# Perceiver block: expert rows scaled two tiles ahead, gathers issued one per transposed tile, fewer warming products

## The reference, cut to what matters

```python
x = x + _L0_ffn_ref(_layernorm(x, axis=-1), routers, W1, W2)
# _L0_ffn_ref: four times, xt of shape (2048, 128):
logits = xt @ router                      # (2048, 16)
probs = jax.nn.softmax(logits, axis=-1)
w, idx = jnp.max(probs, axis=-1), jnp.argmax(probs, axis=-1)
# over the experts i:
h = jax.nn.silu(xt @ w1) @ w2             # 128 -> 512 -> 128
sel = jnp.where(idx == i, w, 0.0)
acc = acc + sel[:, None] * h
```

## Time and profile before

| | us |
|---|---|
| median of three runs | 706.57 |
| lowest, highest | 699.62, 711.03 |
| profiled execution | 701.39 |
| its span, first to last instruction | 699.6 |

### The profile page before, as it was taken

The page is one execution under the profiler, slowest core; times in us unless marked ns, Lnnn a source line. Parts: engine busy times, 40 slices in busy tenths (PEclk is TensorE's granted clock), DMA queues, the critical chain, the costliest instruction groups (busy, mean ns, idle before and its releaser), DMA issues.

```text
span 699.6 us, 16660 instructions
## 1 busy us (share of the span) xinstructions
PE 525.8 (75%) x5941; PEld 438.4 (63%) x5941; DVE 335.9 (48%) x928; ACT 298.5 (43%) x785; POOL 213.8 (31%) x267
## 2 busy tenths in 40 slices
PE   2799999987795479997557799755789885437893
PEld 2477777765462379983456798344679744436893
DVE  3577778775854035564323456522335552113473
ACT  1467677776330156551224455122445412113561
POOL 7323222202026720034720003472000447630053
PEclk9999999999987679999659999967999986658997
DMA  4866666340201200001100000110000101110010
GB/s 119 260 216 202 202 201 203 142 173 2 61 13 50 50 13 2 1 26 40 46 15 1 1 2 25 40 51 13 1 1 2 33 31 51 46 27 1 1 39 24
DMA packets 30079, 42.51 MB, mean 61 GB/s; under 512 B 5552, under 2 KB 23344, under 8 KB 27952
## 3 DMA queue, kind: packets, MB, share of 16 engines
q10 hardware_dynamic: 2304, 17.30, 7.1%
q1 hardware_dynamic: 22576, 13.38, 6.4%
q0 software_dynamic: 5120, 10.76, 5.3%
HBM read 17.70 MB, written 23.72 MB: 59 GB/s over the span
## 4 chain that ended last, share of the span: by engine, by line
PE 52%; issue 16%; DVE 11%; ACT 7%; another core or an unknown queue 6%; POOL 3%; DMA 2%; DVEq 1%; ACTq 0%; POOLq 0%
PE bank L872 15%; PE bank L889 13%; PE bank L691 5%; PE bank L672 4%; ACT pp L579 3%; PE bank L650 2%; PE bank L861 2%; DVE pp L1221 2%; DVE xin L1166 2%; DVE ppT L1005 2%; POOL expert_rows L360 1%; PE bank L644 1%; PE bank L809 1%; PE bank L840 1%
## 5 line engine op out<-in xcount | busy, mean ns | idle before, releaser
L1221 DVE SCALAR_TENSOR_TENSOR pp<-pp,bank 128x512 f32<-128x512 f32 x124 | 85.3, 688 | 217.7 <-ACT pp L579 177.2
L889 PE MATMUL bank<-w,pp 128*128 x992 | 148.9, 297 | 14.9 <-issue 10.5
L872 PE MATMUL bank<-vm,ppT 128*128 x992 | 153.1, 304 | 0.4 <-ACT vm L570 0.4
L889 PEld LDWEIGHTS bank<-w,pp 128*128 128x128 f32 x992 | 132.0, 207 | 20.0 <-issue 17.9
L360 POOL DMA_INDIRECT expert_rows<-yrows,place_i x64 | 62.5, 976 | 261.8 <-DVE place_i L1151 244.8
L872 PEld LDWEIGHTS bank<-vm,ppT 128*128 128x128 f32 x992 | 136.8, 214 | 2.6 <-issue 0.7
L579 ACT ACTIVATE pp<-bank 128x512 f32<-128x512 f32 x124 | 74.2, 598 | 143.1 <-PE bank L872 82.7
L567 ACT COPY ppT<-w 128x512 f32 x124 | 76.7, 619 | 46.7 <-DVE piece_tile L1184 30.5
L861 PE MATMUL bank<-ident,xin 128*128 128x128 f32 x64 | 23.6, 369 | 96.1 <-DVE xin L1166 73.6
L861 PEld LDWEIGHTS bank<-ident,xin 128*128 128x128 f32 x64 | 10.0, 157 | 108.9 <-DVE xin L1166 83.6
L372 POOL DMA_INDIRECT xin<-expert_rows,source_i x64 | 61.1, 955 | 28.1 <-issue 17.7
(11 more groups left out here) (180 smaller groups left out, 635.1 us busy)
## 6 DMA issues: line engine op xcount, KB each, us to landing
expert_rows<-yrows ACTq DMA_DIRECT2D x16, 1056.0 KB, 5.3
w<-in_L_ffn_W_dram SPq DMA_DIRECT2D x32, 256.0 KB, 5.6
cx<-in_ctx_dram SPq DMA_DIRECT2D x16, 128.0 KB, 5.1
x_rows<-xs SPq DMA_DIRECT2D x1, 1024.0 KB, 5.0
expert_rows<-yrows,place_i POOLq DMA_INDIRECT x64
xin<-expert_rows,source_i POOLq DMA_INDIRECT x64
xs<-in_x_dram SPq DMA_DIRECT2D x1, 768.0 KB, 5.9
xs<-in_x_dram SPq DMA_DIRECT2D x1, 256.0 KB, 3.0
```

The lines of the kernel that those rows point to most:

```text
L872: last = mm(banks[2 + j % 2][:, c * P:(c + 1) * P], w1_piece[:, j % 2, c * P:(c + 1) * P], xT[:, ds(tile_of[j] * P, P)], start=True, stop= ...
L889: last = mm(banks[6 + j % 2][:, 0:D], hh[:, j % 2, c * P:(c + 1) * P], w2[:, ds(e * FF + c * P, P)], start=(c == 0), stop=(c == FC - 1))
L1221: v.scalar_tensor_tensor(hh[:, j % 2, :], th[:, j % 2, :], 1.0, banks[2 + j % 2][:, :], ALU.add, ALU.mult).then_inc(s["h_ready"], 1)
```

## The change

Four edits in three engines' lists. On POOL, gather t of a layer for t >= 4 waits until the layer's transposes 0 to t-4 are done, and in layer 3 the gather of x2 row tile t waits until t pieces of the layer have been added. On PE, 2 instead of 8 products are issued ahead of each of the first four `ranks`. On DVE, step i of layers 1 to 3 issues `scale(layer, i + 2)` where it issued `scale(layer, i)`. The work itself stays the same.

```diff
@@ gather_rows (POOL)
                     if t == 0:
                         pool.wait_ge(s["source_ready"], 2 * layer + 1)
                         pool.wait_ge(s["scattered"], (layer + 1) * 16 * NT)
-                    elif t == 4:
-                        pool.wait_ge(s["source_ready"], 2 * layer + 2)
+                    elif t >= 4:
+                        if t == 4:
+                            pool.wait_ge(s["source_ready"], 2 * layer + 2)
+                        pool.wait_ge(s["xT_mm"], layer * NT + t - 3)
@@ finish_rows (POOL)
                 for t in range(NT):
+                    pool.wait_ge(s["y_ready"], (L - 1) * PIECES + t)
                     g.indirect_dma_start(
                         out=yrows[0][:, t, 0:D], out_offset=None, in_=x2_rows,
@@ first routing (PE)
             for q in range(4):
-                stay_warm(banks[7], 8)
+                stay_warm(banks[7], 2)
                 ranks(0, q)
@@ one_layer, step (DVE)
                 def step(i):
-                    if layer > 0 and 2 <= i < NT:
-                        scale(layer, i)
+                    if layer > 0 and i + 2 < NT:
+                        scale(layer, i + 2)
```

## The result

The changed kernel takes 602.87 us (median of 4 runs, 595.55 to 608.64) against 704.44 us before (median of 4), a ratio of 0.854 with a 95% interval of 0.842 to 0.867. 604 us was forecast. The profiled execution took 601.27 us, its span is 599.4.

The account below looks back on a forecast made before the run. Bounds: first halves slowed by late scales and held signals. Gains 2.6 + 11.9 + 27.7 + 26.1 + 31.2 = 99.5 us off 701.39 give 602; splitting the 5.2 us to the runs' median gives 604, range 588 to 642.

Parts of the forecast that it names:

- The scale on the path: Layers 1 to 3, first halves: the late scale idles PE each step, 3.22 us; two tiles ahead gives 1.90.
- Held signals in the unbroken run: First halves: during 16 gathers, one each 1.25 us, PE's results reach other engines late; spacing them loses nothing.
- Rows 6: Layer 0 profile rows read as a product at 238.92 whose tanh began at 248.25, a hold of 8.3 us.
- D: Rival, slower: held transpose signals delay POOL's waiting gathers; whole gain lost at 8.1 us hold, 767 us at 12; chance 0.04.
- Rival A: Spaced gathers still hold PE's signals, 0.92 us per indirect DMA: 648 us, or 626 at half; chance 0.22.
- The added wait and its slack: First halves: the loop from transpose to product takes about 3.9 us, leaving 1.8 us to spare at 1.90 a step.
- Warming products: Ahead of the first four ranks: six fewer products at 0.43 us each gain 2.6 us.
- Layer sums: First halves: layer 0 falls from 43.1 to 31.2 us, layers 1 and 2 from 60.5 and 58.9 to 32.8.
- x2 gathers: Layer 3: their run stays nearly unbroken and costs 13 us; the layer still gains 31.2.
- rival B: Layer 3's x2 gathers cost nothing: 591 us; chance 0.14.
- rival C: The clock stays low through the first halves, 3.8 us a step: 698 us, no change; chance 0.03.
- the sign of being wrong that the prediction named last: Layers 1 to 3: the first gathers, an unbroken run of about six, already hold signals once PE is faster.

Follow-up runs that it names:

- experiment 2: Kernel before, with only the gathers of xin from the fourth on tied to the transposes: 662.8 us, ratio 0.938.
- experiment 1: Kernel before, with only the scale issued two tiles ahead: 653.2 us against 706.7, ratio 0.924.
- experiment 5: Changed kernel with a POOL memset ahead of each gather from gather 4 on, replacing the wait for a transpose: 606.0 us, ratio 0.855.
- experiment 7: Changed kernel plus 24 plain loads from SP in each layer once gather 7 has landed: 605.6 us, ratio 0.854.
- experiment 10: Changed kernel with gathers from gather 4 on let go in fours, same mean rate: 624.1 us, ratio 0.887.
- Experiment 6: Changed kernel with gather t waiting for transpose t-2 instead of t-4: 637.6 us, ratio 0.899.
- experiment 9: Changed kernel with the gather of x2 tile t waiting for t+9 added pieces instead of t: 600.5 us beside 597.3.
- experiment 4: Changed kernel without the new wait on the gathers of x2 rows: 597.7 us, measured once.
- experiment 8: Changed kernel without x2 gathers: SP writes the residual into the output and the last 16 scatters add to it: 593.1 us, ratio 0.838.

## Why the prediction was right, point by point

- *The scale on the path.* Right: steps of 3.22 became 1.90 us, and experiment 2 keeps 3.22 where the scale stays late.
- *Held signals in the unbroken run.* Right, and the step on which most hung. Experiments 1, 5, 7 and 10 place it: it goes with POOL's indirect DMAs at 1.25 us apart, not with DMA traffic, POOL's being busy or the tie to PE. Not every signal in such a run is late. In layer 1 before the change (timeline):

```profile
341.50 2.00 PE L872 MATMUL bank<-vm,ppT 128*128 x8
...
343.33 0.94 POOL L372 DMA_INDIRECT xin<-expert_rows,source_i  x1 [0.30 <-issue]
343.54 0.60 ACT L579 ACTIVATE pp<-bank 128x512 f32<-128x512 f32 x1 [1.53 <-PE bank L872]
...
344.58 0.94 POOL L372 DMA_INDIRECT xin<-expert_rows,source_i  x1 [0.30 <-issue]
```

This product ended 10 us into the run of 16 gathers and its tanh began at once; the next one's began 5.5 us late. What decides which signal is held is open. Rows 6 were paired wrongly, too: by the order of the program the tanh at 248.25 belongs to the product at 234.47, which ended at 236.38, and that of 238.92 began at 250.65. So the hold was 11.9 and 10.7 us, not 8.3. No term of the sum hung on it, but D's threshold did. Rival A, a price for each DMA, fell: at 1.77 to 1.90 us apart the price is zero. What inside the chip holds the signal no run shows. The Trainium skill in "SBUF — State Buffer" (SBUF: two separate sides) says that engine and DMA ports are disjoint and that PE never waits on anyone. That speaks of ports, and nothing here contradicts it: inside the runs a hidden product at the full clock still took 1.06 us (540.40 above, 347.28 in experiment 1), and late was what the other engines saw of its end. The prediction was wrong to set the page against the trace.

- *The added wait and its slack.* Right: POOL waited 36 times, DVE's scale never for it. Experiment 6 measured the loop where it binds: 2.6 us a step as worked out. So D needed a hold, and the wait prevents it.
- *Warming products.* 2.6 us was forecast, 2.3 us measured at an equal clock; another 1.6 to 2 us in the profile were the logits' clock.
- *Layer sums.* Too small a gain: 31.2, 32.8 and 32.8 us forecast, 29.3, 30.2 and 30.7 measured. In layers 1 and 2 the step that was off is the clock's return: I let three steps run at the lower clock, but after 2.30 and 3.39 us layer 1 went at 1.90. In layer 0 it was a hold that I didn't see. I kept the second step at its size, but it fell from 4.45 to 2.69 us, and the same product ran at full clock in both (1.06 us at 238.92 before). Before the change the first tanh was held:

```profile
232.39 2.07 PE L872 MATMUL bank<-vm,ppT 128*128 x8 [0.42 <-ACT vm L570]
...
236.26 0.60 ACT L579 ACTIVATE pp<-bank 128x512 f32<-128x512 f32 x1 [3.09 <-issue]
```

It began 1.8 us after its product's end (234.46), after the change at once (239.16 against 239.12), and in both kernels the third product follows it by 2.66 us.

- *x2 gathers.* "Nearly unbroken" is right, the new wait caught two of 16. Its price was 16.3 us (8.83 + 10.63 + 2.39 less 1.95 and twice 1.79), I took 13. It lay partly outside the first half: the halves' window of layer 3 is 36.7, not 46, and the rest follows in the window after it. That layer 3 gained 30.8 us, as good as the 31.2 forecast, is two errors that cancel. With this price rival B is out, and rival C too: the windows show a clock of 0.87 to 0.94 in the first halves, and in layer 1 only the first two hidden products ran at the lower one.
- *Not foreseen:* the first gather to the first product of layer 0 took 6.5 instead of 4.7 us. The signal of the first transpose came 3.0 us after its end, before the change 1.2, right behind 16 scatters and beside gathers 0 to 3:

```profile
233.22 0.47 PE L864 MATMUL bank<-ident,xin 128*128 128x128 f32 x1 [11.61 <-DMA xin<-expert_rows,source_i]
...
236.65 0.27 ACT L573 COPY vm<-bank 128x128 f32<-128x128 f32 x1 [15.62 <-remote]
```

This is the sign of being wrong that the prediction named last, the first gathers holding signals; it came in layer 0 and not in layers 1 to 3. POOL's gap was to stand before each gather from the fifth on, 48 in all; it stands before 36, nine a layer. The waits for scaled rows fell to 18.3, not under 10 us; they are the layers' starts.

- *The sum.* 602 us for the profiled execution, 601.3 measured, is closer than the terms deserve, and that is luck: the change gained 107.9 us instead of 99.5, and the untouched front part took 7.7 us more.

## What to carry to other kernels

Look how closely indirect DMAs follow each other while TensorE feeds other engines: give each its place between the steps that use it (here one per transposed tile), for a run at full rate can cost more than the transfers. When a wait is added for that, add up its whole loop against the steps it spans; a lead of four tiles was free here, two cost 0.7 us a step. When a run of them can only be moved, as in experiment 9, the loss moves along: remove the DMAs instead.

## What the runs showed of the hardware

- A TensorE product's completion reached ACT's tanh up to 15.1 us after its end by the profile while POOL issued indirect DMAs 1.25 us apart (before 11.9, experiment 1 14.0, experiment 4 16.4). In the four runs shown above the tanh began 0.9 to 2.9 us after the last issue had ended; others began while a run still went on. Beside gathers, scatters and adding scatters 1.77 us apart and more no tanh waited more than 0.5 us for its signal (experiments 5, 7 and 8). In experiment 8 the latest of all, 2.2 us, stand at the layers' ends beside four scatters in a run.
- Plain loads from SP at a 35% share of the DMA engines held nothing.
- An indirect scatter of 128 rows of 512 bytes kept POOL busy for 0.96 us, one that adds for 1.56 us.
- Runs as short as four are enough: 1.7 to 3.2 us at their ends (experiment 10). Yet at the start of layer 1 there, eight gathers in a run held no tanh, and neither of the first two tanhs in the run of 16 in layer 1 before the change was late.
- A transpose's signal is held too: 15.7 us in experiment 1, 3.0 us after the change, in layer 0.
